# A mixture-of-experts block on one core: the high part of each weight rounded on chip by GpSimd, in place of a second, converting fetch

## What is computed

```python
x = x + tanh(g_xattn) * attention(layernorm(x), ctx, 16 heads of 16)
t = layernorm(x)
logits = t @ gate_w.T                      # 8 experts, the best 2 of each row are used
h = gelu(t @ W1[e] + b1[e])                # 256 -> 1024, for each chosen expert e
y = h @ W2[e] + b2[e]                      # 1024 -> 256
out = sum of the two y by their shares + gelu(t @ sW1 + sb1) @ sW2 + sb2   # shared expert
x = x + tanh(g_ffn) * out
```

## Time and profile before

| | us |
|---|---|
| median of the runs | 598.15 (596.72, 598.15, 605.92) |
| the profiled execution | 592.66 |
| span of its profile | 591.0 |
| attention, up to the last logits | about 213 |
| early tiles and scatter | about 213 to 266 |
| routed tiles | about 266 to 541 |
| late tiles, gather and store | about 541 to 591 |

### The profile page before, as it was taken

One profiled execution on the slowest core, in us unless ns is written; L12 is line 12 of the kernel. 1 busy time (PEld: TensorE's weight loads), 2 busy tenths in 40 slices (PEclk: granted clock), 3 DMA queues, 4 the chain that ended last, 5 costly groups with the idle time before them and its releaser, 6 DMA issues.

```text
span 591.0 us, 12133 instructions
## 1 busy us (share of the span) xinstructions
PE 530.8 (90%) x3143; PEld 461.2 (78%) x3144; DVE 372.7 (63%) x771; ACT 241.0 (41%) x528; POOL 230.5 (39%) x177
## 2 busy tenths in 40 slices
PE   4915999868899869999999999999999999999995
PEld 3615888858888758888888888888888888888884
DVE  3463577787768468666655566555655556555888
ACT  2203556454556443343344343433334333343431
POOL 8032225341500006774415443444444444301773
PEclk9957788897989869999999999999999999999999
DMA  7776355653576222324667665736776667111453
GB/s 237 184 207 206 96 152 161 211 165 94 147 226 215 90 97 99 124 107 142 188 205 203 211 188 183 225 115 204 200 237 178 216 175 224 48 37 55 136 175 122
DMA packets 75421, 95.86 MB, mean 162 GB/s; under 512 B 6469, under 2 KB 63236, under 8 KB 75404
## 3 DMA queue, kind: packets, MB, share of 16 engines
q0 software_dynamic: 23712, 57.18, 32.0%
q1 hardware_dynamic: 44316, 32.44, 18.2%
q10 hardware_dynamic: 7376, 6.03, 3.5%
HBM read 68.15 MB, written 20.71 MB: 150 GB/s over the span
## 4 chain that ended last, share of the span: by engine, by line
PE 60%; POOL 10%; DVE 9%; issue 9%; DMA 5%; ACT 4%; SPq 1%; DVEq 1%; POOLq 0%; ACTq 0%
PE ps L645 13%; PE ps L632 7%; PE ps L633 7%; PE ps L634 7%; PE ps L646 7%; PE ps L620 6%; POOL gath L564 5%; POOL routed_x L528 5%; PE ps L702 3%; PE ps L688 3%; PE ps L659 2%; PE ps L613 2%; DMA moved_q<-hid 1%; DMA qstack<-moved_q 1%; DVE xres L1126 1%
## 5 line engine op out<-in xcount | busy, mean ns | idle before, releaser
L645 PE MATMUL ps<-w2hl,hTh 128*128 (+1 forms) x440 | 161.6, 406 | 2.9 <-DVE hTl L1142 2.9
L646 PE MATMUL ps<-w2hl,hTl 128*128 (+1 forms) x440 | 123.6, 281 | 0.0
L992 ACT ACTIVATE hid<-hid 128x512 f32<-128x512 f32 x110 | 69.3, 632 | 131.5 <-DVE hid L1148 131.4
L645 PEld LDWEIGHTS ps<-w2hl,hTh 128*128 128x128 f32 x440 | 82.7, 188 | 20.4 <-issue 3.5
L986 ACT ACTIVATE hTh<-ps 128x512 fp32r<-128x512 f32 x110 | 60.0, 597 | 94.4 <-PE ps L620 94.4
L1148 DVE TENSOR_TENSOR hid<-ps,b1bc 128x512 f32<-128x512 f32 x110 | 75.3, 689 | 29.7 <-PE ps L634 24.7
L632 PE MATMUL ps<-w1l,xT 128*128 (+1 forms) x220 | 92.5, 420 | 0.0
L633 PE MATMUL ps<-w1h,xT 128*128 (+1 forms) x220 | 87.5, 398 | 0.0
L634 PE MATMUL ps<-w1h,xT 128*128 (+1 forms) x220 | 87.2, 396 | 0.0
L646 PEld LDWEIGHTS ps<-w2hl,hTl 128*128 128x128 f32 x440 | 83.0, 189 | 0.0
L1142 DVE TENSOR_TENSOR hTl<-ps,hTh 128x512 fp32r<-128x512 f32 x110 | 70.8, 685 | 0.2
(11 more groups left out here) (160 smaller groups left out, 782.0 us busy)
## 6 DMA issues: line engine op xcount, KB each, us to landing
stage<-in_L_ffn_W POOLq DMA_DIRECT2D x16, 1024.0 KB, 6.1
w1h<-in_L_ffn_W POOLq DMA_DIRECT2D x8, 1024.0 KB, 5.8
w2hl<-in_L_ffn_W POOLq DMA_DIRECT2D x8, 1024.0 KB, 7.9
qstack<-moved_q SPq DMA_DIRECT2D x48, 128.0 KB, 2.4
xrow<-routed_x SPq DMA_DIRECT2D x39, 128.0 KB, 2.1
routed_y<-yrow ACTq DMA_DIRECT2D x39, 128.0 KB, 1.7
routed_x<-zeros SPq DMA_DIRECT2D x6, 768.0 KB, 3.9
moved_q<-hid SPq DMA_DIRECT2D x16, 256.0 KB, 2.3
```

The costliest lines, as they stand in the source:

```text
L645: mm(p_y, hTh[:, c, :], part(2 * D), start=c == 0, stop=False)
L646: last = mm(p_y[:, 0:D], hTl[:, c, :], part(D), start=False, stop=c == FC - 1)
L992: act.activation(hid[:, n, :], hid[:, n, :], ACT.Gelu).then_inc(S["h_act"], 1)
```

## The change

`load_hi1` and `load_hi2` go, with the semaphores `w1h_in` and `w2h_in`. In their place GpSimd rounds the staged original itself: `round_w1` and `round_w2` wait for the stage, copy it to the float32r buffer (128 x 2048 elements) and raise a semaphore (`w1h_set`, `w2h_set`), and `split_w1` and `split_w2` wait for that one and then subtract as before. So each of the 20 splits has one copy on GpSimd ahead of it, and 20 transfers of 1 MB are gone. Nothing else is moved.

```diff
-            def load_hi1(s, src):
-                pool.dma_start(w1h[:, bass.ds(s, 1), :, :].rearrange("p o c f -> p (o c) f"), src
-                               ).then_inc(S["w1h_in"], 16)
-
-            def load_hi2(s, src):
-                pool.dma_start(w2hl[:, bass.ds(s, 1), :, 0:D].rearrange("p o c f -> p (o c) f"), src
-                               ).then_inc(S["w2h_in"], 16)
+            def round_w1(p, s):
+                pool.wait_ge(S["stage1_in"], 16 * p + 16)
+                met(pool)
+                hi = w1h[:, bass.ds(s, 1), :, :].rearrange("p o c f -> p (o c) f")
+                pool.tensor_copy(hi, stage1[:]).then_inc(S["w1h_set"], 1)
 
             def split_w1(p, s):
-                pool.wait_ge(S["stage1_in"], 16 * p + 16)
-                pool.wait_ge(S["w1h_in"], 16 * p + 16)
+                round_w1(p, s)
+                met(pool)
+                pool.wait_ge(S["w1h_set"], p + 1)
...
+            def round_w2(p, s):
+                pool.wait_ge(S["stage2_in"], 16 * p + 16)
+                met(pool)
+                both = w2hl[:, bass.ds(s, 1), :, :].rearrange("p o c f -> p (o c) f")
+                pool.tensor_copy(both[:, :, 0:D], stage2[:]).then_inc(S["w2h_set"], 1)
...
             load_w1(0, sW1_v)
             key_diag(2)
-            load_hi1(0, sW1_v)
             load_w2(0, sW2_v)
             key_diag(3)
-            load_hi2(0, sW2_v)
             split_w1(0, 0)
...
-            load_hi1(1, expert_w1(0))
             key_diag(6)
-            load_hi2(1, expert_w2(0))
             split_w1(1, 1)
...
                 pool.wait_ge(S["h_add"], halves)
-                load_hi1(s, here[0])
                 load_b1(s, bias[0])
                 split_w1(p, s)
...
                 pool.wait_ge(S["y_sum"], first)
-                load_hi2(s, here[1])
                 load_b2(s, bias[1])
                 split_w2(p, s)
```

More of the change, by code:

```diff
@@ L256, in gated_cross_attention_and_moe @@
             route tiles_set chosen_set rank_ps share_in share_tanh tables_set slots_set scattered
-            stage1_in stage2_in b1_in b2_in w1h_in w2h_in split_w1 split_w2 w1_ready w2_ready
+            stage1_in stage2_in b1_in b2_in w1h_set w2h_set split_w1 split_w2 w1_ready w2_ready
             xT_ps xT_hi xT_lo h_ps h_add h_act hT_ps hT_hi hT_lo y_ps y_mid y_sum y_done y_stored
@@ L449, in split_w1 @@
                 pool.wait_ge(S["split_w1"], p + 1)
+            def round_w2(p, s):
[3 more added lines that the diff above has]
+                pool.tensor_copy(both[:, :, 0:D], stage2[:]).then_inc(S["w2h_set"], 1)
             def split_w2(p, s):
-                pool.wait_ge(S["stage2_in"], 16 * p + 16)
-                pool.wait_ge(S["w2h_in"], 16 * p + 16)
+                round_w2(p, s)
+                met(pool)
+                pool.wait_ge(S["w2h_set"], p + 1)
                 both = w2hl[:, bass.ds(s, 1), :, :].rearrange("p o c f -> p (o c) f")
```

## The result

| | kernel before | changed kernel |
|---|---|---|
| median of the comparison, us | 599.09 (12 runs, 593.72 to 605.92) | 602.31 (12 runs, 599.45 to 605.28) |
| ratio of the executions compared | 1 | 1.013, 95% interval 1.0105 to 1.0155 |
| span of the profiled execution, us | 591.0 | 601.0 |
| last logits done (GpSimd's `tile_i`), us | 213.7 | 220.2 |
| from there to the end, us | 377.3 | 380.8 |

The changed kernel is slower by 3 us by the medians and by 10 us by the two traces; both are under 2%.

What follows compares the result with a forecast made beforehand. TensorE was taken as the bound, busy 274.38 of 275.00 us in the routed tiles; only the attention could move the end. Holds 4.9, clock 2, transfers -3 gave +3.9 on 598.15, so 602 us, range 594 to 609.

Steps and rivals of the forecast that it cites:

- holds in the attention: Attention: four copies each delay a split that VectorE meets; changed holds sum to +4.9 us.
- clock: Attention: three splits add a hold and one is relieved, each followed by 1.1 us of slow TensorE; +2, bounds 0 and 3.3.
- transfers and queries: TensorE's 5.05 us stop at 54.55: one of two 1 MB weights in flight goes; gain 3 us, bounds 1 and 5.05.
- routed tiles: Eight phases: TensorE has no gap, VectorE's lines read PSUM, GpSimd loses waits longer than nearly any copy price; cost 0.
- Price of a copy: X, the time of one GpSimd copy: taken as 2.5 us, kept between 1.8 and 4.5.
- 4X - 5.1: Sum of changed holds at the attention's four splits, X being one copy's time: 4.9 us at X = 2.5.
- The wait between copy and split: GpSimd waits for its own result after a copy; taken as 0.57 us, as behind a split.
- X - 0.2: First and second attention splits: added hold of L1126 at each, X being one copy's time.
- One input is enough: Whether a GpSimd copy with one input also holds the port pair against VectorE; the prediction said no row shows it.
- Rival A, the copy keeps the port: First and third attention copies: the queued copy goes before waiting VectorE; +8.8 us, 607, at X = 2.5; 15%.
- A hold is paid in full: Attention: a held VectorE instruction lengthens the step by its whole hold, and up to a microsecond over.

Runs made afterwards that it cites:

- one fetch later: Kernel before, with the second fetch of the first weight (1 MB) issued behind the fourth sequence's `key_diag`, 20 us later; 597.48 us against 597.65, ratio 1.0043.
- phase 2 held back: Changed kernel, with GpSimd waiting for the last early tile's result (`y_done`) before phase 2; 598.57 us against 595.56 for the kernel before, ratio 1.0097.
- double dose: Changed kernel with each of the attention's four copies done twice; 604.88 us against 597.65 for the kernel before, ratio 1.0131.

## Why the prediction was right or wrong

The forecast was 602 us within 594 to 609, no change by 2%, and a cost of 3.9 us. Measured were 602.31 us and +3.2 by the medians, +5 if all executions of both kernels in the comparisons are taken together (about 597 and 602), +10 by the traces. The direction was right, and so was the mechanism of the holds, place by place. That the sum came out near is in part luck: the net holds were taken too large, the clock too small, and a cost in the routed tiles was missing. Term by term, against the first pair of traces:

| term | predicted, us | first pair of traces, us |
|---|---|---|
| holds in the attention | +4.9 | +0.6 |
| clock | +2 | +4.4 in the 11 steps, +5.5 behind them |
| transfers and queries | -3 | -2.8 up to the second marked step (clock included), -1.3 at 169.73 |
| routed tiles | 0 | +2.4 |
| tile period, not counted as the change's | none | +1.0 |
| sum | +3.9 | +10 |

**Price of a copy.** Taken as 2.5 us, measured 1.90 to 1.95; the term of the holds was mis-sized by it first of all (4X - 5.1 is 2.6 at 1.93, not 4.9). The write-only instruction (1.81) was the right neighbour; the split's two reads do not divide into equal shares. (The prediction gives 4.53 us for all splits; those of the loop take about 4.6.) The Trainium skill's "GPSIMD Engine Reference", section 3.1, has 1.03 cycles an element for a body with at most two operations, from which the prediction worked out an estimate of 1.8 us a copy. With that the trace nearly agrees.

**The wait between copy and split.** Taken as 0.57 us, it was 0.15 in three of four places and 0.54 at the third, where `x2row` ran in it.

**The holds.** The place and the line were right in all four. With X = 1.93: first L1126 held 1.64 us (its 2.13 less 0.49), of which 0.5 was there before: +1.1 came where X - 0.2 gives 1.7; second +2.0 against 1.7; third -3.5 against -3.4; fourth +2.0 against 2.5. Sum +1.6 where 4X - 5.1 gives 2.6 at 1.93. Beside these the shift of the work took one hold of 2.06 us off `xn` (the one at 106.58) and put one of 1.1 on `x2row` at 112.79, so that with all small ones the net is +0.6. The step that fails is the one that took the holds of the other `key_diag` as fixed. The run with one fetch later shows the same in the open.

**One input is enough.** No row had shown a copy against VectorE; `x2row` at 133.29 was held 0.54 us, until 0.26 before the copy's recorded end. The Trainium skill's "SBUF — State Buffer", section "SBUF: two separate sides", lets a GpSimd instruction and a VectorE one in a 2-port mode contend for the pair, and makes no exception for a copy with one input. By that rule the trace agrees.

**Rival A, the copy keeps the port.** Refuted: `xn` at 129.92 ended at 132.34, as `key_diag` ended, though the copy stood next in GpSimd's queue; it took 2.42 us, 2.44 in the kernel before.

**Clock.** In the 11 steps, 3.7 us of difference, less 0.6 of net holds and with the 1.3 us of the stop that went, leave 4.4 where 2 was taken and 3.3 was the bound. The 5.5 us behind 196 us were in no term. The step that failed was to price the clock per hold, at the place of the hold.

**Transfers.** A gain of 3 was taken; the stop fell by 1.4 us and the first step by 2.6, clock included. Traces with one weight in flight scatter from no stop to 4.79 us. The size was right, the certainty was not. And the sentence that the other transfers shorten nothing that TensorE waits for missed the stop of 1.3 us at 169.73: no transfer was taken away there, but the copy put the weight's load behind the queries.

**Routed tiles at no cost.** Wrong, +2.4 us in this trace and +3.8 in the second, where the granted clock also fell to half for 3.4 us behind the same wait of TensorE. I had looked for VectorE's lines that read PSUM and left out L1267, which ran once more behind the start of the loop. The prediction asked what hides an added instruction, but not what the removed wait had kept apart: 4.15 us of waiting for the transfer had put the split behind L1267. The runs with copies in the attention alone and with phase 2 held back take it away in two ways.

**"A hold is paid in full."** The dose agrees: about 2 us more of copy at three places made the 11 steps 5.3 to 7.1 us longer. One trace of the double dose is all there is.

## What to carry to other kernels

When a wait for a transfer is taken away, ask which two instructions it had kept apart, and look through every line of the other engine that could now meet the one that moved up, in the last turn of a loop too. Where VectorE and GpSimd share work in SBUF, put GpSimd's instructions behind a signal from VectorE at the start of a stretch that reads only PSUM: here that turned a loss of 3 to 5 us into a gain of 10, and moving the first loads out of the way of small transfers, with the splits a slot later, made it 17. Where the chain between the engines has TensorE pause often, add the time at the low clock to the balance: here it was more than the holds themselves. In a chain of short steps every microsecond of shift moves later meetings, so a gain read at one place has to be followed to the end of the stage before it is counted.

## What the hardware did that I had not expected

- TensorE's clock, down behind a pause of 2.65 us that all kernels have, stayed at 0.50 (1.2 GHz) for 10.2 to 17.1 us in five of five traces of one group, for 6.8 in one and for 3.4 in the seven others, under the same instructions of TensorE. Cost 3.4 to 5.5 us in the five.
- GpSimd's next instruction comes 0.13 to 0.25 us behind a copy whose result it waits for. Behind a split the next fetch comes 0.56 to 0.59 us later in the attention and 0.08 to 0.17 in the loop. Why the two differ is open.
- An execution of one program on one core scatters from 587 to 607 us, while both traces of the kernel before have spans of 591 and 592. The granted clock goes with it: in the kernel before its mean is 0.932 to 0.948 in the 17 executions under 594 us and 0.912 to 0.935 in the 18 above 601 (of 65 whose clock is known). Where in the program it falls in the longer ones is open, as none of them was traced.
